# Cross attention of a Perceiver block: keys made in fp32 a head pair ahead, and scores taken as queries times keys

## The reference, cut to what matters

```python
q = (hidden_states @ Wq).reshape(B, Sq, H, D)          # H = 16 heads, D = 128
k = (encoder_hidden_states @ Wk).reshape(B, Skv, H, D)
v = (encoder_hidden_states @ Wv).reshape(B, Skv, H, D)
q = rmsnorm(q, gq)
k = rmsnorm(k, gk)
scores = jnp.einsum('bqhd,bkhd->bhqk', q, k) * scale
attn = jax.nn.softmax(scores, axis=-1)
out = jnp.einsum('bhqk,bkhd->bqhd', attn, v)
return out.reshape(B, Sq, H * D) @ Wo
```

## Time and profile before

| | us |
|---|---|
| median of 3 executions | 980.36 (979.6 to 980.44) |
| the profiled execution: device time | 985.37 |
| the profiled execution: span of the page and of all rows | 983.6 |
| TensorE (PE) busy | 951.0 (97%) |
| VectorE (DVE) busy | 681.6 (69%) |
| ScalarE (ACT) busy | 591.0 (60%) |
| GpSimd (POOL) busy | 273.9 (28%) |
| chain that ended last: share of TensorE | 67% |

### The profile page before, as it was taken

The page is one execution under the profiler, slowest core; times in us unless marked ns, Lnnn a source line. Parts: engine busy times, 40 slices in busy tenths (PEclk is TensorE's granted clock), DMA queues, the critical chain, the costliest instruction groups (busy, mean ns, idle before and its releaser), DMA issues.

```text
span 983.6 us, 20438 instructions
## 1 busy us (share of the span) xinstructions
PE 951.0 (97%) x6572; PEld 812.7 (83%) x6573; DVE 681.6 (69%) x1053; ACT 591.0 (60%) x966; POOL 273.9 (28%) x170
## 2 busy tenths in 40 slices
PE   9999799999999999999999999899999999999996
PEld 7888698989988887788888887777788888888885
DVE  6655665676567765667777774756577888788876
ACT  6544676666667656455555634441377787778773
POOL 2200231332123052223333300000223544544441
PEclk9999999999999999999999999999999999999999
DMA  9100453331233241122222007111488889999995
GB/s 313 62 1 1 103 193 108 107 82 40 91 107 121 21 131 53 64 86 85 85 85 95 11 21 253 55 43 60 177 303 276 282 276 336 349 326 299 301 332 164
DMA packets 76146, 145.12 MB, mean 148 GB/s; under 512 B 13540, under 2 KB 41060, under 8 KB 75856
## 3 DMA queue, kind: packets, MB, share of 16 engines
q1 hardware_dynamic: 68256, 132.53, 39.9%
q0 software_dynamic: 7856, 12.16, 5.4%
HBM read 146.86 MB, written 15.07 MB: 165 GB/s over the span
## 4 chain that ended last, share of the span: by engine, by line
PE 67%; DMA 10%; SPq 9%; issue 7%; DVE 4%; ACT 2%; DVEq 0%; ACTq 0%; POOLq 0%
PE ps L328 18%; PE ps L330 17%; PE ps L329 17%; PE ps L730 6%; DMA w_and_lists<-in_w 5%; SPq L983 4%; DMA w_raw<-in_w 2%; SPq L1224 2%; PE ps L1016 2%; PE ps L717 1%; SPq L1228 1%; SPq L1227 1%; PE ps L815 1%; DMA xe<-xn_scratch,take 1%; PE ps L799 1%
## 5 line engine op out<-in xcount | busy, mean ns | idle before, releaser
L1041 DVE TENSOR_TENSOR w_l<-w_raw,w_h 128x1408 fp32r<-128x1408 f32 x76 | 122.1, 1624 | 34.6 <-ACT w_h L1037 19.6
L1037 ACT ACTIVATE w_h<-w_raw 128x1408 fp32r (+1 forms) x76 | 103.1, 1376 | 39.7 <-DMA w_raw<-in_w 34.5
L760 POOL TENSOR_TENSOR lw_l<-lw_raw,lw_h 128x1024 fp32r<-128x1024 f32 x32 | 77.4, 2433 | 133.6 <-ACT lw_h L756 128.7
L328 PE MATMUL ps<-w_h,xeT_h 128*128 128x352 f32 x288 | 97.7, 339 | 5.5 <-DVE w_l L1041 4.8
L329 PE MATMUL ps<-w_l,xeT_h 128*128 128x352 f32 x288 | 93.0, 323 | 0.0
L330 PE MATMUL ps<-w_h,xeT_l 128*128 128x352 f32 x288 | 92.9, 323 | 0.0
L1197 POOL DMA_INDIRECT xe<-xn_scratch,take x37 | 39.5, 1067 | 185.0 <-DVE give L1145 102.2
L1201 POOL DMA_INDIRECT y_scratch<-ob,give x34 | 80.7, 2373 | 21.9 <-issue 9.7
L328 PE MATMUL ps<-xT_hi,lw_h 128*128 128x512 f32 x192 | 77.9, 406 | 0.3
L329 PE MATMUL ps<-xT_lo,lw_h 128*128 128x512 f32 x192 | 76.0, 396 | 0.0
L330 PE MATMUL ps<-xT_hi,lw_l 128*128 128x512 f32 x192 | 76.0, 396 | 0.0
(11 more groups left out here) (327 smaller groups left out, 2677.8 us busy)
## 6 DMA issues: line engine op xcount, KB each, us to landing
w_raw<-in_w SPq DMA_DIRECT2D x78, 704.0 KB
w_and_lists<-in_w SPq DMA_DIRECT2D x39, 512.0 KB
w_and_lists<-in_w SPq DMA_DIRECT2D x39, 192.0 KB
rkB<-rk_scratch SPq DMA_DIRECT2D x56, 128.0 KB, 3.2
wq_raw<-in_Wq SPq DMA_DIRECT2D x8, 512.0 KB, 5.2
wo_raw<-in_Wo SPq DMA_DIRECT2D x16, 256.0 KB, 5.4
lw_raw<-in_kwT SPq DMA_DIRECT2D x8, 512.0 KB, 3.3
lw_raw<-in_qwT SPq DMA_DIRECT2D x8, 512.0 KB, 3.4
```

The lines of the kernel that those rows point to most:

```text
L328: nc.tensor.matmul(out_ap, lh, rh, start=first, stop=False)
L760: e.tensor_tensor(lw_l[n][:, :, :], lw_raw[n][:, :, :], lw_h[n][:, :, :], ALU.subtract).then_inc(lw_ready[n], 1)
L1037: e.activation(w13_h[:, k, n, :, :], w13_raw[:, slot(raw), n, :, :], ACT.Copy).then_inc(w13_hi_s, 1)
L1041: e.tensor_tensor(w13_l[:, k, n, :, :], w13_raw[:, slot(raw), n, :, :], w13_h[:, k, n, :, :], ALU.subtract).then_inc(w13_ready, 1)
```

## The change

The keys stage goes, and so do the weight-folded queries. In its place each pair of heads makes the keys of the pair ahead: eight blocks (four chunks of 512 context tokens for each of two heads), six matmuls of 512 columns each, with the weights as the stationary and the context as the moving operand. VectorE copies each block into `kT` in plain f32, ScalarE squares the copy (`ksq`), and TensorE sums the squares over the head dimension in `xa_pe_ss`, with 32 columns of `ksq` as weights and one column of ones moving: 128 matmuls for the keys and 32 for the queries, all into single columns of one bank. `rms` and its reciprocal `rqk` now hold 8 columns for the queries and 32 for the keys. The 32 are transposed (`xa_pe_rkT`), copied, stored to the scratch and read back once for each pair. The queries stay plain f32 (`qn`), and a score block is `qn` times `kT`: a matmul for each head and batch, 64 columns of weights, 256 moving columns, head 0 on PSUM partitions 0 to 63 and head 1 on 64 to 127.

The order in a pair changes on all engines. TensorE: scores, queries ahead, keys ahead, sums of squares, output projection of the pair before, the small transpose, then transposes of probabilities and `xa_pe_u` as before, and `xa_pe_ao` at the end.

The core of the diff:

```diff
@@ helpers @@
+        def xa_act_ksq(e, p, n):
+            c, k = n // 2, n % 2
+            e.wait_ge(kT_ready, p * NK + (n + 1))
+            e.activation(ksq(n), kT[:, k, c * G4:(c + 1) * G4].rearrange("p (a n) -> p a n", a=2), ACT.Square,
+                         scale=RS4).then_inc(ksq_ready, 1)
+
+        def xa_dve_kT(e, p, n):
+            e.wait_ge(k_ps, p * NK + (n + 1))
+            e.tensor_copy(kT[:, n % 2, n // 2 * G4:(n // 2 + 1) * G4], ps[:, KB[n], :]).then_inc(kT_ready, 1)
...
+        def xa_pe_key(e, p, n):
+            c, k = n // 2, n % 2
+            tk = slice(c * G4, (c + 1) * G4)
+            for a in range(CC):
+                m = mm3(ps[:, KB[n], :], wk_h[:, a, hcol(k)], wk_l[:, a, hcol(k)], cT_h[:, a, tk], cT_l[:, a, tk],
+                        a == 0, a == CC - 1)
+            m.then_inc(k_ps, 1)
+
+        def xa_pe_keys(e, i):
+            p = i + 1
+            e.wait_ge(wk_ready, p + 1)
+            for n in range(NK):
+                if n < 2 and isinstance(i, int) and i == 0:
+                    e.wait_ge(rkT_ready, 1)
+                elif n < 2:
+                    e.wait_ge(ao_split, i * 2)
+                elif n < 6:
+                    e.wait_ge(s_ready, i * 4 + (n - 1))
+                else:
+                    e.wait_ge(kT_ready, p * NK + (n - 5))
+                xa_pe_key(e, p, n)
+
+        def xa_pe_ss(e, p):
+
             e.wait_ge(sq_ready, p * 2 + 2)
+            e.wait_ge(kT_ready, p * NK + NK)
+            e.wait_ge(ksq_ready, p * NK + NK)
+            for n in range(NK):
+                for s in range(4):
+                    col = B + n % 2 * KT + n // 2 * 4 + s
+                    for r in range(4):
+                        at = s % 2 * P + r * Q4
+                        m = e.matmul(ps[r * Q4:(r + 1) * Q4, SSB, col:col + 1], ksq(n)[:, s // 2, at:at + Q4],
+                                     ones[:, 0:1], start=True, stop=True)
...
         def xa_pe_scores(e, i, j):
             if j == 0:
-                e.wait_ge(qp_ready, i * 4 + 4)
+                e.wait_ge(qn_ready, i * 2 + 2)
             for n, b in enumerate((2 * j, 2 * j + 1)):
-                for c in range(CC):
-                    m = mm3(ps[:, SB[j], n * SKV:(n + 1) * SKV],
-                            qpT_h[:, c, b, :, :].rearrange("p k q -> p (k q)"), qpT_l[:, c, b, :, :].rearrange("p k q -> p (k q)"),
-                            cT_h[:, c, kvb(b)], cT_l[:, c, kvb(b)], c == 0, c == CC - 1)
+                for k in range(2):
+                    m = e.matmul(ps[k * SQ:(k + 1) * SQ, SB[j], n * SKV:(n + 1) * SKV], qn[:, k, b * SQ:(b + 1) * SQ],
+                                 kT[:, k, kvb(b)], start=True, stop=True)
             m.then_inc(s_ps, 1)
@@ SyncE @@
+            def rk_store(p):
+                e.wait_ge(rkT_ready, p + 1)
+                e.dma_start(rk_w[bass.ds(p, 1)].rearrange("h r n -> (h r) n"), rkT[:, :]).then_inc(rk_out, 16)
+                e.wait_ge(rk_out, p * 16 + 16)
...
+            with e.Fori(1, HP - 2) as i:
+                wk_load(i + 2)
+                wq_load(i + 2)
+                wv_load(i + 1)
+                rk_load(i + 1)
+                pair_out(i + 1)
@@ TensorE @@
-            for t in range(KT):
-                keys(0, t, True)
-            with e.Fori(1, 3) as g:
-                for t in range(KT):
-                    keys(g, t)
+            e.wait_ge(wk_ready, 1)
+            for n in range(NK):
+                if n % 2 == 0:
+                    e.wait_ge(cT_ready, n // 2 + 1)
+                if n >= 6:
+                    e.wait_ge(kT_ready, n - 5)
+                xa_pe_key(e, 0, n)
             for t in range(TT):
+                if t < 2:
+                    e.wait_ge(kT_ready, t + 5)
                 ln_tile_pe(e, 0, t, xn_a)
-            for t in range(KT):
-                keys(3, t)
             e.wait_ge(xT_ready, TT)
             xa_pe_q(e, 0, 0)
...
             xa_pe_q(e, 0, 1)
             xa_pe_ss(e, 0)
...
+            def pair(i, y=None):
                 for j in range(JB):
...
                     xa_pe_scores(e, i, j)
+                if isinstance(i, int) and i == 0:
+                    xa_pe_rkT(e, 0, 6)
+                xa_pe_q(e, i + 1, 0)
+                xa_pe_q(e, i + 1, 1)
+                xa_pe_keys(e, i)
+                xa_pe_ss(e, i + 1)
                 if y is not None:
                     xo_pe(e, y)
...
+                xa_pe_rkT(e, i + 1, 5)
+                xa_pe_pT(e, i, 0)
+                xa_pe_pT(e, i, 1)
                 xa_pe_u(e, i, 0)
                 xa_pe_pT(e, i, 2)
+                e.wait_ge(rkT_ready, i + 2)
                 xa_pe_u(e, i, 1)
                 xa_pe_pT(e, i, 3)
                 xa_pe_u(e, i, 2)
                 xa_pe_u(e, i, 3)
-                if more:
-                    xa_pe_qp(e, i + 1)
                 xa_pe_ao(e, i)
```

More of the change, by code:

```diff
@@ L397, in perceiver_block @@
         AO = H + 2
[L400 removed]
+        YB = (0, 1, 2, 3)
         YL = (2, 3, 0, 1)
@@ L438, in xo_pe @@
                     e.wait_ge(s_ready, (i + 1) * 4 + t + 1)
+                if not last and t < 2:
+                    e.wait_ge(kT_ready, (i + 2) * NK + (4 + t + 1))
+                if not last and t >= 2:
+                    e.wait_ge(qn_ready, (i + 2) * 2 + (t - 1))
                 xo_pe_tile(i, t, YL[t] if last else YB[t])
@@ L682, in xa_pe_ss @@
             for b in range(B):
-                for n in range(4):
-                    m = e.matmul(ps[n * Q4:(n + 1) * Q4, 2 + b // 4, b % 4 * P:b % 4 * P + Q4],
-                                 sq[:, b, n // 2, n % 2 * Q4:(n % 2 + 1) * Q4], ones[:, 0:Q4], start=True, stop=True)
+                for r in range(4):
+                    m = e.matmul(ps[r * Q4:(r + 1) * Q4, SSB, b:b + 1],
+                                 sq[:, b, r // 2, r % 2 * Q4:(r % 2 + 1) * Q4], ones[:, 0:1], start=True, stop=True)
@@ L1546, in _, with pair @@
             xa_act_q(e, 0, 0)
-            e.wait_ge(small_ps, PS_RKT)
-            for n in range(2):
-                e.activation(rkT[:, n, :], ps[:, 6 + n, 0:P], ACT.Copy).then_inc(rkT_ready, 1)
             xa_act_q(e, 0, 1)
+            xa_act_wq(e, 1)
             xa_act_rms(e, 0)
-            xa_act_qp(e, 0)
-            def pair(i, more):
-                if more:
-                    xa_act_weights(e, i + 1)
+            xa_act_wk(e, 1)
+            def pair(i, more=True):
                 xa_act_exp(e, i, 0)
@@ L1576, in pair @@
                 xa_act_u(e, i, 3)
-                if more:
-                    xa_act_qp(e, i + 1)
+                xo_act_weights(e, i)
                 xo_act_heads(e, i)
-            pair(0, True)
-            with e.Fori(1, HP - 1) as i:
-                pair(i, True)
+            pair(0)
+            with e.Fori(1, HP - 2) as i:
+                pair(i)
+            pair(HP - 2, False)
             def last_pair(i):
@@ L1701, in _ @@
                     ln_mean_var(e)
[L1702 to L1705 removed]
+            ln_tiles_inverse(e, 0, TT, 1)
+            for t in range(TT):
+                ln_tile_scale(e, t, xn_a)
             e.wait_ge(g_in_s, 32)
             e.tensor_tensor(gqk[:, 2:3], gqk[:, 0:1], gqk[:, 1:2], ALU.mult).then_inc(small_dve, 1)
[L1708 to L1710 removed]
@@ L1724, in _ @@
             xa_dve_rq(e, 0)
-            xa_dve_qp(e, 0)
-            def pair(i, more, y=None):
+            xa_dve_rkT(e, 0, 6)
+            def pair(i, y=None):
                 e.wait_ge(soft_step, i * SOFT + 1)
```

393 lines of the change are left out of this document (150 added, 243 removed).

## The result

The changed kernel takes 1042.38 us (median of 4 executions, 1039.71 to 1042.73), the kernel before 980.4 beside it (979.6 to 981.12). The ratio is 1.0627, 95% interval 1.0607 to 1.0646. The prediction was 1007 with a range of 988 to 1038: the sign was right, the size was not, and the time lies 4 us outside the range. The profiled execution of the changed kernel took 1042.17, with a span of 1040.4, 56.8 more than the span before.

The account below looks back on a forecast made before the run. TensorE's work was taken to bound each pair, now 44.45 instead of 31.96. Pair 0's earlier start -46.7, pairs 1 to 6 +74.8, last pair -1.4: +26.7 in all, 1007 us, range 988 to 1038.

Parts of the forecast that it names:

- rival 2: Scores: the two halves do not run side by side at 256 columns; +3.6 in eight pairs, +25, 1032; chance 0.05.
- rival 1: Sums of squares: 0.031 per record, 9.8 instead of 3.2; +53, at half +26, 1033 to 1060; chance 0.10.
- the row with four column groups: Trace row used to price the sums of squares: 64 records of 32 weight columns in 0.69, giving 3.2 for 320.
- (a): Wait in front of `xa_pe_ss`, behind the keys, for the last copy and its square: 1.65 a pair.
- (b): Wait for `u_h`, `u_l` in front of `xa_pe_ao`, no longer covered by weight-folded queries: 1.7 a pair.
- (c): Wait of `xa_pe_u` for the copy of the first transposes, which the sums of squares covered before: 0.3 a pair.
- rival 3: Not slower: the three waits in TensorE's queue don't open; 3.65 in seven pairs, 25.6, giving 981.5; chance 0.08.
- Rival 4: Shorter start: clock doesn't fall, layer norm earlier, pair 0's key factors sooner; -8 to -10, 998; within own case's 0.77.
- the prediction's estimate of 8 us: Cost of the 320 sum records by the skill page's 25 ns floor; the prediction took 3.2 instead.
- the term for the sums of squares: `xa_pe_ss` on TensorE: 320 records in place of 64, taken as 3.2 a pair, bounds 2 and 9.8.
- the rivals of price: Dearer sums of squares (rival 1) and scores (rival 2); half of the first plus the second set the upper end, 1038.
- one of the two f32 prices: Sign for a steady pair's period: 48 or more would mean an f32 price was wrong; 44 to 45 was expected.

Follow-up runs that it names:

- experiment 2: Changed kernel with the output projection of the pair before issued ahead of the sums of squares, so no idle time precedes them; 1019.3 us, ratio 1.0389.
- experiment 6: Changed kernel with 12 moving columns instead of one in each of the 320 sum records; 1027.15 us, ratio 1.0489.
- experiment 7: Changed kernel with both the output projection issued ahead of the sums and twelve moving columns in the sum records; 1010.4 us, ratio 1.0302.
- experiment 1: Kernel before, with its query sums issued five times: 320 records of 32 moving columns per pair; 1019.81 us, ratio 1.0399.
- experiment 3: Changed kernel without the 128 key-sum products, four matmuls filling their columns (key factors wrong in value), the wait kept; 1004.55 us, ratio 1.0244.
- experiment 10: Changed kernel with key squares in fp32r, summed by matmuls of 512 columns with a block of ones; key-factor transpose, store and load gone; 995.07 us, ratio 1.0155.
- experiment 4: Changed kernel with the key sums cut into portions of 32 records, each put behind a later key block; 1026.99 us, ratio 1.0468.
- experiment 8: Kernel before, with its query sums issued ten times: 640 records of 32 moving columns per pair; 1132.15 us, ratio 1.1539.
- experiment 9: Kernel before, with its query sums issued ten times, one moving column each: 640 records per pair; 1136.76 us, ratio 1.1616.

## Why the prediction was wrong, step by step

Where the spans differ, 56.8, against the forecast of 26.7: 2.5 at the start, 6.8 in pair 0, 6.8 in pair 1, five times 3.17 in pairs 2 to 6, and 2 less behind them, 30 in all. The medians differ by 5 more than the spans, because the profiled execution before lay 5.0 above its median and the one after did not.

**What held.** Scores: 3.60, forecast 3.6, so rival 2 is out. Queries and keys: 5.70 and 11.2, forecast 5.49 and 10.95. The tiny records: 0.0083 each at full clock, 2.77 for the 320 (experiment 2), forecast 3.2 and inside its bounds, so rival 1 is out, although the total lies where that rival had it (1033 to 1060); the row with four column groups was the right one, that with two was not. Waits: (a) 1.53 for 1.65, (b) 1.5 for 1.7, and (c) 0.25 for 0.3; rival 3 is out, the waits open and stay. With the clock repaired (experiment 6) the pair is 44.8 against 44.45. First product of scores on VectorE: 14.5 behind the first scores (61.61 after 47.10), forecast 13.7. The way to the first queries: VectorE's one-column product waits beside POOL's split again (28.05, for 2.33), the queries begin at 32.83, forecast 33.3, and run at 0.50 until 36.1, which costs about the 1.5 forecast. Rival 4 is out too: 47.10 is later, not earlier.

That one column costs as much as 60, as the Trainium skill has it ("TensorEngine Tiling (Array Packing)", Performance Considerations), agrees with these runs as far as they go: records of 1, 12 and 32 moving columns cost the same. The distance does not: 0.0083 a record, with 32 columns of weights each, is a third of the 25 ns behind the prediction's estimate of 8 us.

**What failed, first: the clock.** The prediction took the steady pair at full clock and looked for 0.50 only between 28 and 38, since it read the earlier trace rows as the effect of idle time. The step that failed is the term for the sums of squares, which was priced by its duration alone. It has a second price: 2.8 in each pair (0.6 in the burst, the rest in the ten products after it), 14 of the 15.9 us that pairs 2 to 6 are over. Experiments 6 and 7 show that it goes from the steady pairs when the same records move twelve columns.

"TensorE: Matmul & The Clock Gate", Part 1, of the Trainium skill lets the clock follow how busy the engine was. Read with the PE column that would predict no fall here, and the trace does not agree: in experiment 2 PE is busy for all of the burst and of the 1.0 us behind it, and the clock falls there; in experiment 6 the same records with the same wait, but twelve columns, keep it at 1.00.

**What failed, second: the first passes.** The prediction sums what the engines do, and the rows of the kernel before, whose bursts are 64 records long, show no pause at them. Here there are five: 2.3 in the start, 1.65 and 1.85 in pair 0, 1.87 and 1.58 in pair 1. They explain the start's 2.5, and 3.5 of the 6.8 in each of the two pairs. In pair 1 the rest is the clock, about 3 us of it. In pair 0 the granted clock is 0.50 from 77.15 to 90.90; held against the same instructions in a steady pair, that costs 1.5 in the burst, 0.7 in eight transposes and 1.6 in 16 products, which with the pauses is 0.5 more than the 6.8. That the pauses belong to the tiny records is shown by experiments 1 (they appear in the old kernel), 3 and 10 (gone with the records), 4 (gone in pair 1 when the records are spread), 8 and 9 (there in every pair of a longer loop). That they are waits for instruction packets is argued from the 128 records between two of them and from the packet counts, and not shown by a run.

**What failed, third: the range.** It was made wide by the rivals of price and not at all by a fall of the clock in the pairs. The signs had the same gap: 44 to 45 was the forecast, 48 or more meant one of the two f32 prices, and 47.6 stood for nothing.

Slips in the working change the total by some 0.2 us at most. 31.96 a pair should be 31.99 and 139.20 should be 139.04. What a pair gains beside the moved keys is 6.3 by the prediction's own terms, not 6.5, so TensorE's work shrinks by some 17 us, not 15.

What stays open is what exactly lowers the clock. These are the stretches that were seen, and nothing between them was tried:

| ahead of the full-size products | clock in steady pairs |
|---|---|
| 1.5 idle, 320 records of 1 column | falls in the burst |
| no idle, 320 of 1 column | falls 1 us behind it |
| 1.5 idle, 72 records (64 of 1 column) | falls 1 us behind it (not in pair 1) |
| no idle, 320 of 1 column, in the kernel before | fell in two pairs of five |
| no idle, 64 of 1 column | 1.00 |
| no idle, 32 of 1 column at a time, eight times | 1.00 |
| 1.5 idle alone | 1.00 |
| 1.5 idle, 320 of 12 columns | 1.00 |
| no idle, 320 of 12 columns | 1.00 |
| no idle, 320 of 32 columns | 1.00 |

The second and the fourth line have the same burst, but the clock falls in every steady pair of the first and in two of five of the second. What stands around the burst matters, then, and that was not isolated.

## What to carry to other kernels

Price a burst of tiny matmuls three times: its records, the clock of what comes behind it, and its instructions on the first passes or in a long loop. Here the records cost 2.77 a pair, the clock 2.8 in a steady pair, and the pauses 3.5 in each of the first two. Where tiny matmuls can't be avoided, try a dozen moving columns, which cost nothing more here (0.0084 a record for 0.0083) and kept the steady pairs at 1.00, or use one wide product with a block of ones. Scattering them between large products took the pauses of pair 1 and the fall away, but each change of shape cost about 0.1 us on either side, 2.2 a pair.

## What was not expected of the hardware

- One-column matmuls at 0.0083 us each leave the engine busy by its records and the granted clock at 0.50 from the burst on, for about 7 us in the changed kernel (271.7 to 278.4). The same records with twelve columns left it at 1.00 in the steady pairs.
- Instructions come in packets of 16 KB, by the counts 128 matmuls with their weight loads. Tiny ones use up as many in 1.1 us at 0.0083 each, and TensorE pauses 1.6 to 2.3 us in the changed kernel, up to 5.0 in experiment 1. A loop of 543 matmuls ran without pauses, and all but without packets, from the second pass on; one of some 850 did not.
- f32 products of 256 columns in two column halves run side by side: 3.60 for 32 records, 0.11 each, where a record of 512 columns over the full width took 0.46, so 0.23 for half the columns.
- Going from matmuls with 128 weight columns to ones with 32 or 64 and back cost about 0.1 at each edge, 0.28 for a portion of 32 records.
